# Transposes among the products, a later place for the softmax transposes, and a stage change that awaits no store

## What is computed

```python
x = L0_attn_x
xn = _layernorm(x, axis=-1)
s = _L0_attn_ref(xn, ...)          # four heads of 128 columns, concatenated, @ warboss_w + warboss_b
g = _silu(_L0_ffn_ref(xn, ...))    # relu(xn @ w1 + b1) @ w2 + b2, w1: 512x2048, w2: 2048x512
x = x + s * g

def _full_attention(x, qkv_w, scale):            # local head
    qkv = x @ qkv_w
    q, k, v = jnp.split(qkv, 3, axis=-1)
    scores = jnp.einsum('bsh,bth->bst', q, k) * scale
    probs = jax.nn.softmax(scores, axis=-1)
    return probs @ v
# sparse head: the same, but scores below the row's 102nd largest are masked before the softmax
# memory head: softmax(x_proj @ bank.T) over 64 entries, then [x_proj, retrieved] @ mem_out_w + b
# prediction head: two linear layers, exact gelu, one linear layer
```

## Time and profile before

| | us |
|---|---|
| median of 3 runs (2620.21 to 2622.47) | 2621.97 |
| the profiled execution | 2622.3 |
| its span in the profile | 2620.5 |
| TensorE busy | 2536.6 (97%) |
| VectorE busy | 2308.1 (88%) |
| ScalarE busy | 1367.2 (52%) |
| GpSimd busy | 1101.9 (42%) |

### The profile page before, as it was taken

How to read it: one execution, slowest core, us unless ns; L and a number is a source line. 1 busy time by engine, 2 the same in 40 slices (tenths; PEclk the granted TensorE clock), 3 DMA queues, 4 the chain that set the end, 5 groups by cost and what they waited for, 6 DMA issues and landing times.

```text
span 2620.5 us, 37059 instructions
## 1 busy us (share of the span) xinstructions
PE 2536.6 (97%) x12900; PEld 2145.1 (82%) x12900; DVE 2308.1 (88%) x5217; ACT 1367.2 (52%) x2311; POOL 1101.9 (42%) x863
## 2 busy tenths in 40 slices
PE   6999999969999999999999999999999999999998
PEld 5887888857888888888888888888888888888886
DVE  7555555569999999999999999999999999999996
ACT  5777777734444445444444444544455444445443
POOL 4444444423344444444444444444444444444444
PEclk9999999989999999999999999999999999999999
DMA  6777777794556455655664556456655655475554
GB/s 215 291 291 296 286 273 273 291 349 145 195 185 239 164 193 197 227 175 195 203 232 162 193 199 227 165 197 216 209 183 179 239 187 199 164 243 175 196 169 166
DMA packets 168554, 562.29 MB, mean 215 GB/s; under 512 B 18160, under 2 KB 31664, under 8 KB 159920
## 3 DMA queue, kind: packets, MB, share of 16 engines
q1 hardware_dynamic: 168368, 559.91, 61.1%
HBM read 425.63 MB, written 134.22 MB: 214 GB/s over the span
## 4 chain that ended last, share of the span: by engine, by line
PE 75%; DVE 2%; DMA 1%; POOL 0%; issue 0%; ACT 0%; SPq 0%; POOLq 0%
PE acc L58 9%; PE acc L59 9%; PE acc L60 9%; PE hid L60 9%; PE hid L58 9%; PE hid L59 9%; PE o L58 4%; PE o L60 4%; PE o L59 4%; PE scores L1250 4%; PE scores L60 2%; PE scores L58 2%; PE scores L59 2%; DVE larger L1166 1%; DVE top_l L1146 1%; DMA xnT<-xnT_scratch 0%
## 5 line engine op out<-in xcount | busy, mean ns | idle before, releaser
L1006 POOL TENSOR_TENSOR h_lo<-h,h_hi 128x512 fp32r<-128x512 f32 x256 | 332.5, 1299 | 876.0 <-ACT h_hi L904 874.9
L1146 DVE MAX8 top_l<-larger 128x8 f32<-128x512 f32 x832 | 573.9, 690 | 13.2
L1166 DVE MATCH_REPLACE8 larger<-top_l,larger 128x512 f32<-128x512 f32 x768 | 519.3, 676 | 0.0
L903 ACT ACTIVATE h<-hid,b 128x512 f32<-128x512 f32 x256 | 176.4, 689 | 484.5 <-PE hid L60 484.0
L58 PE MATMUL acc<-w2s,h_hi 128*128 128x512 f32 x1024 | 411.7, 402 | 0.0
L58 PE MATMUL hid<-xnT,w1s 128*128 128x512 f32 x1024 | 399.6, 390 | 4.9 <-DMA w1s<-ffn_scratch 2.0
L59 PE MATMUL acc<-w2s,h_hi 128*128 128x512 f32 x1024 | 400.3, 391 | 0.0
L60 PE MATMUL acc<-w2s,h_lo 128*128 128x512 f32 x1024 | 400.3, 391 | 0.0
L60 PE MATMUL hid<-xnT,w1s 128*128 128x512 f32 x1024 | 399.8, 390 | 0.0
L59 PE MATMUL hid<-xnT,w1s 128*128 128x512 f32 x1024 | 399.0, 390 | 0.0
L1006 POOL TENSOR_TENSOR pT_s<-pT,pT_s 128x512 fp32r<-128x512 f32 x256 | 326.3, 1296 | 50.9 <-ACT pT_s L916 50.9
(11 more groups left out here) (170 smaller groups left out, 5570.8 us busy)
## 6 DMA issues: line engine op xcount, KB each, us to landing
w2s<-ffn_scratch SPq DMA_DIRECT2D x259, 512.0 KB, 3.9
w1s<-ffn_scratch SPq DMA_DIRECT2D x258, 512.0 KB, 4.5
kv<-kv_scratch SPq DMA_DIRECT2D x34, 1024.0 KB, 6.6
xnT<-xnT_scratch SPq DMA_DIRECT2D x68, 512.0 KB, 7.6
tl<-tile_scratch SPq DMA_DIRECT2D x66, 512.0 KB, 3.9
xnT_scratch<-xnT SPq DMA_DIRECT2D x16, 2048.0 KB, 13.6
kv_scratch<-kv_out SPq DMA_DIRECT2D x32, 1024.0 KB, 5.6
tile_scratch<-tiles_out SPq DMA_DIRECT2D x16, 2048.0 KB, 7.7
```

The costliest lines, as they stand in the source:

```text
L903: nc.scalar.activation(h32[:, c % 2, :], hid[:, :], ACT.Relu, bias=bias)
L1006: return nc.gpsimd.tensor_tensor(out_, value, hi_.bitcast(F32), ALU.subtract).then_inc(ready, 1)
L1146: l_step = count(nc.vector.max(top_l[:, own], larger[:, :]))
L1166: l_step = count(nc.vector.match_replace(larger[:, :], top_l[:, own], larger[:, :], LOWEST))
```

## The change

**Stage 1.** `JOBS` has a new order: `tr0` stands behind `ql`, `tr1` behind `qs`, `tr2` behind `kl`, and `wt` behind `ks`. Each of these four jobs of transposes is woven into the last three matmuls of the job before it: one transpose before them, one in each of the two gaps, one behind. VectorE makes `gelu_lo` before it splits the result of `wt`. The last step drops the load and the layer norm of a half batch that nobody reads and the load of an `ffn` chunk; VectorE makes the last low part of `v23` in GpSimd's place.

**The change of stages.** `xnT`, and one buffer each for the first tile, the sparse head's keys and the first `w1` chunk, are now shared by both stages. Stage 2 finds its first `xnT` half there, and the three others are loaded in the last step of stage 1, before its last two stores. SyncE waits for the landing of the `xnT` stores only at the end of stage 1; for `tile_scratch` and `kv_scratch` it waits inside stage 2, in front of the loads that read them (`load_kv` of the local keys, `load_tl`) or later. Further loads of `xnT` are issued one slot later.

**Stage 2.** `f2` takes the transposes and puts one behind the first and one behind the second of the three matmuls of each product, eight in all. `tr_done` now counts halves, and ScalarE waits for each half. The last group of all stays as it was.

```diff
-JOBS = ["mp", "pi", "ql", "ms", "p1a", "p1b", "qs", "wt", "kl", "ks", "p2",
-        "tr0", "tr1", "tr2", "tr3", "mo", "v01", "v23"]
+JOBS = ["mp", "pi", "ql", "tr0", "ms", "p1a", "p1b", "qs", "tr1", "kl", "tr2", "ks", "wt", "p2", "tr3", "mo",
+        "v01", "v23"]
+WOVEN = {"ql": "tr0", "qs": "tr1", "kl": "tr2", "ks": "wt"}
...
+def woven(nc, out, w_hi, w_lo, x_hi, x_lo, first, last, between):
+
+    nc.tensor.matmul(out, w_hi, x_hi, start=first, stop=False)
+    next(between, None)
+    nc.tensor.matmul(out, w_hi, x_lo, start=False, stop=False)
+    next(between, None)
+    return nc.tensor.matmul(out, w_lo, x_hi, start=False, stop=last)
...
-    LO = ["xp", "pin", "wt", "gelu"]
+    LO = ["xp", "pin", "gelu", "wt"]
...
+                def load_first():
+
+                    sp.wait_ge(kv_st, 32 * LAST)
+                    sp.wait_ge(tiles_st, 16 * LAST)
+                    loads = ((shared.tl0[:, :, :, :].rearrange("p i s n -> p (i s n)"),
+                              tile_d[0, :, :, :, :].rearrange("p i s n -> p (i s n)")),
...
+                    for (to, of), ready in zip(loads, shared.first_in):
+                        sp.dma_start(to.bitcast(F32), of).then_inc(ready, 16)
...
+                        if n == LAST:
+                            load_first()
...
-                        load_ffn((n + 1) & (CH - 1))
-
-                        sp.wait_ge(kv_l, 4 * n + 4)
+                        if n < LAST:
+                            load_ffn(n + 1)
+                            sp.wait_ge(kv_l, 4 * n + 4)
+                        else:
+                            sp.wait_ge(kv_l, 4 * n + 3)
+                            sp.wait_ge(last_v_l, 1)
                         store_kv(2)
...
                 sp.wait_ge(xnT_st, 16 * 2 * B)
-                sp.wait_ge(kv_st, 16 * 4 * B)
-                sp.wait_ge(tiles_st, 16 * 2 * B)
-                sp.wait_ge(ffn_st, 16 * 2 * B)
-                sp.wait_ge(ffn_in, 32 * (2 * B + 1))
...
+                                if name in WOVEN:
+                                    between = one_by_one(n, WOVEN[name])
+                                    next(between)
+                                    last = woven(nc, dst, wp_hi[:, k, c], wp_lo[:, k, c], xnT[:, hh, k, HI, :],
+                                                 xnT[:, hh, k, LOW, :], False, True, between)
+                                    last.then_inc(job_done, 1)
+                                    next(between)
+                                    continue
...
-                load_tl(0, 0, 0)
-                load_kv(U_KS, 0)
-                load_w1(0, 0)
-                load_xn(0, 0, 0)
                 load_w1(1, 1)
+                sp.wait_ge(tiles_st, 16 * 2 * B)
+                load_w2(0, 0)
                 load_kv(U_KL, 0)
-                for c in range(W2_RING - 1):
-                    load_w2(c, c)
+                load_w2(1, 1)
                 load_tl(1, 1, 1)
+                sp.wait_ge(kv_st, 16 * 4 * B)
...
                     i = 2 * g + t
-                    act.wait_ge(tr_done, i + 1)
                     for j in range(2):
+                        act.wait_ge(tr_done, 2 * i + j + 1)
...
-                        last = product(nc, acc[:, t, :], h_hi[:, c % 2, t * P:(t + 1) * P],
-                                       h_lo[:, c % 2, t * P:(t + 1) * P], w2[:, r, HI, :], w2[:, r, LOW, :],
-                                       start, c % CH == CH - 1)
+                        last = woven(nc, acc[:, t, :], h_hi[:, c % 2, t * P:(t + 1) * P],
+                                     h_lo[:, c % 2, t * P:(t + 1) * P], w2[:, r, HI, :], w2[:, r, LOW, :],
+                                     start, c % CH == CH - 1, between)
```

More of the change, by code:

```diff
@@ L13 @@
 from contextlib import ExitStack
+from dataclasses import dataclass
 import concourse.bass as bass
@@ L554, in transposes, with one_by_one @@
                     return last
+                def one_by_one(n, name):
+                    bk = bank(n, name)
+                    free = bank_free(n, name)
+                    if free is not None:
+                        pe.wait_ge(bank_read, free)
+                    if name == "wt":
+                        pe.wait_ge(wn_ready, n + 1)
+                    elif name == "tr0":
+                        pe.wait_ge(xn_ready, n + 2)
+                    for t in range(HTILES):
+                        source = we[:, t, :, :] if name == "wt" else xn[:, t, int(name[2]) * P:(int(name[2]) + 1) * P]
+                        last = nc.tensor.transpose(ps[:, bk, t * P:(t + 1) * P], source, ident[:, :])
+                        if t == HTILES - 1:
+                            last.then_inc(job_done, 1)
+                        yield last
                 pe.wait_ge(consts, CONSTS)
@@ L648, in _, with stage2 @@
                     steps(b)
-def stage2(nc, x, xnT_d, kv_d, tile_d, ffn_d, ident, ww_hi, ww_lo, b2, half_bias, b1, out):
+def stage2(nc, x, xnT_d, kv_d, tile_d, ffn_d, shared, out):
+    ident, ww_hi, ww_lo = shared.ident, shared.ww_hi, shared.ww_lo
+    b2, half_bias, b1 = shared.b2, shared.half_bias, shared.small[:, 0:CH]
+    xnT = shared.xnT
     HC = CH // HTILES
@@ L668, in sem @@
             return ctx.enter_context(nc.semaphore(name))
-        xnT = sb("xnT", [P, 2, KT, 2, HALF], F32R)
-        kv = sb("kv", [P, 8, 2, HALF], F32R)
-        tl = sb("tl", [P, TL_RING, 2, 4, P], F32R)
-        w1 = sb("w1s", [P, W1_RING, 2, D], F32R)
+        values = sb("values", [P, 4, 2, HALF], F32R)
         w2 = sb("w2s", [P, W2_RING, 2, D], F32R)
+        kl = sb("kl", [P, 2, 2, HALF], F32R)
+        units = {U_KS: shared.ks, U_KL: kl, U_VL: values[:, 0:2, :, :], U_VS: values[:, 2:4, :, :]}
+        tl = [shared.tl0] + [sb(f"tl{j}", [P, 2, 4, P], F32R) for j in range(1, TL_RING)]
+        w1 = [shared.w10, sb("w1_1", [P, 2, D], F32R)]
         h32 = sb("h32", [P, 2, HALF], F32)
@@ L1347, in slots @@
                             pe.wait_ge(pl_ready, m + 1)
[L1348 to L1349 removed]
+                            f2(C + 1, c + 1, h, transposes(0))
                             f1(C + 3, c + 3, h)
```

185 lines of the change are left out of this document (110 added, 75 removed).

## The result

The changed kernel takes 2657.3 us (2656.4 to 2659.7), the kernel before on the same chip 2621.1 us: a ratio of 1.0141, 95% interval 1.0123 to 1.0158. It is slower by 36 us, outside the predicted range of 2594 to 2636; the forecast was 2621.2, no change. The profiled execution has a span of 2654.6 us, against 2620.5 before, so 34.1 us are to be found in the two traces.

A forecast was written before the change was run, and what follows sets the result against it. TensorE was taken as the bound, always busy in stage 2, with 22.0 us of stage-1 waits and 17.2 us between stages. 2622.3 + 8.2 - 14.4 + 5.1 = 2621.2 us, range 2594 to 2636.

The forecast's parts named there:

- Part 1: Stage 1: the wait for `we` goes, a 1.9 us wait at `mo` comes; +8.2 us, bounds 0 and +16.
- VectorE's 0.69: Stage 1: VectorE's subtraction on the `wt` result, ahead of `mo`, was taken to last 0.69 us.
- rival D: Stage 1: the wait in front of `mo` lets TensorE's clock fall, 16 x 1.6 = 26 us more, 2647; chance 0.09.
- Part 2: Change of stages: the gap shrinks until transfers become the limit; -14.4 us, bounds -10 and -17.2.
- E+20.6: Change of stages: summed transfers let the second-chunk `w1` product start 20.6 us after TensorE's stage-1 end, 14.3 us earlier.
- keep its length: Early stage 2: the chain through ScalarE's `prob` and TensorE's 4.24 us idle before the transposes stay as long, only moving earlier.
- first `kv` store of the sum: Change of stages: the transfer sum starts with this store, issued 7.3 us before TensorE's end of stage 1.
- Part 3: Stage 2: weaving transposes between products gains nothing, 0.04 us more for each of 127 groups; +5.1 us, bounds -4 and +13.
- The argument for the group: Stage 2: each transpose leaves one weight load bare, eight in a row or woven; group 3.68 us for 3.64.
- Rival B: Stage 2: weaving pays, a woven transpose costs only its columns; 50 us less, 2566; chance 0.09.
- Rival C: Stage 1: the new wait at `mo` does not come, so the 22.0 us are saved; 2592; chance 0.12.

The follow-up runs named there:

- the kernel with 1.69 us: Changed kernel with TensorE's wait at `mo` put behind the three products of `mo` that do not need its result: 2640.3 us.
- e3_old_jobs: Changed kernel with stage 1 in its old job order and nothing woven there; stage change and stage 2 kept: 2620.6 us, 0.9997 of before.
- e10_before_wt_behind_kl: Kernel before with `wt` one place later, behind `kl`, and `gelu_lo` ahead of it on VectorE: 2594.9 us, 0.9904 of before.

## Why the prediction was wrong

**Part 1, stage 1: the wait moved as forecast, and two terms of its price failed.** Stage 1 was to cost 8.2 us and cost 40.1. The two terms are VectorE's subtraction, put at 0.69 us, and the fall of the clock, put at nothing in the forecast. The forecast had the wait for `we` go and one at `mo` come. Its path holds nearly to the end. Counted from the step's start at 297.21, ScalarE begins `qs` at 16.29 (forecast 16.26), VectorE begins its subtraction at 320.69 - 297.21 = 23.48 (23.4), and TensorE reaches `mo` at 322.26 - 2.47 - 297.21 = 22.58 (22.4). The first term that failed is "VectorE's 0.69": it was 1.42, because the later `wt` meets GpSimd's `ks`. 0.73 more there make the result come at 25.05 instead of 24.27, the wait 2.47 instead of 1.9, and a step with full clock 32.42 instead of 31.64. Over 16 steps this is 12.5 us of the miss. The 0.69 was read from a row in which GpSimd was all but done. Its timeline there:

```profile
325.81 1.29 POOL L315 TENSOR_TENSOR tiles_out<-tiles_out 128x512 fp32r<-128x512 f32 x1 [6.13 <-ACT tiles_out L408]
```

It ends at 327.10, 0.11 us after VectorE's start. The trace of before had the warning in its groups by line and form (busy, mean ns of one). Two groups of subtractions of one shape cost 929 and 690 ns on the mean: half of the first meet a running operation of GpSimd and take up to 1.54 us, none of the second does:

```profile
L447 DVE TENSOR_TENSOR xnT<-xnT 128x512 fp32r<-128x512 f32 x56 | 49.9, 929 | 64.8 <-ACT xnT L433 64.8
...
L447 DVE TENSOR_TENSOR act_lo<-act,act_hi 128x512 fp32r<-128x512 f32 x30 | 20.7, 690 | 14.4 <-ACT act_hi L378 14.4
```

**The second term is the clock: rival D had the mechanism and was given 0.09.** It put 1.6 us on a fall; 1.5 was measured, 13 times instead of 16, some 19 us, and its sign, a granted clock under 1.00 in stage 1, is there (0.96). The step that failed was to set the point of decision between 1.4 and 4.24 us and then weigh it as if it lay near the upper end. Nothing between the two had been seen, so a wait of 1.9 was an open case, and the kernel with 1.69 us shows that the clock would have fallen about every second time. With a wait that long and a fall in half of the steps, the forecast of 2621 would have been some 12 us too low even without VectorE's 0.73.

**Part 2, the change of stages: nearly right.** Forecast -14.4, bounds -10 and -17.2. The timeline of TensorE in the changed kernel, which answers to the earlier trace rows:

```profile
569.95 0.56 PE L60 MATMUL scores<-ks,tl 128*128 128x512 f32 x1 [2.95 <-PEq L228]
...
580.01 0.47 PE L60 MATMUL hid<-xnT,w 128*128 128x512 f32 x1 [4.11 <-DMA w<-ffn_scratch]
...
587.84 0.50 PE L60 MATMUL hid<-xnT,w 128*128 128x512 f32 x1 [0.52 <-DMA w<-ffn_scratch]
...
623.25 0.79 PE L67 MATMUL acc<-w2s,h_hi 128*128 128x512 f32 x1 [5.59 <-ACT prob L1030]
```

TensorE ends stage 1 at 567.0, the forecast's E. The product that was summed up to E+20.6 stands at 587.84, E+20.8 (it opens the third chunk of the hidden layer and not the second, in both kernels). Behind it the wait for `prob` is 5.6 and not the 4.24 that was to "keep its length", and up to the fifth slot 13.3 us are won. In e3_old_jobs, whose stage 1 is that of before, it is only 9.6, just outside the bounds. There TensorE waits 5.1 us for `ks` and 4.0 for `w1`, and the former is shorter in the changed kernel (2.95). SyncE's timeline of the changed kernel has the reason, and it makes the hit at E+20.6 a lucky one:

```profile
557.31 0.36 SPq L305 DMA_DIRECT2D kv_scratch<-kv_out  x1
```

This is the first `kv` store of the sum, 9.7 us before E; the forecast said 7.3, and in e3_old_jobs it is 6.4. From it to the product at the end of the sum it is 30.5 us in both kernels, and 27.9 in the forecast. So the transfers took 2.6 us longer than they were summed to, and the stores had 2.4 more of a start, because E itself was put off by the late subtraction and the fall of the clock (0.8 and 1.5 us).

**Part 3, the weaving: right in sign and in the group, low in sum.** Forecast +5.1, upper bound +13; the 28 pairs show +8.3, the kernel without weaving 7 us less. The group of 8 and 12 was to take 3.68 and takes 3.68. What was left out lies behind it: in the 12 products of the next chunk the 11 distances add up to 0.038 us more, 2.531 for 2.493 on the mean of 87 groups from 1000 to 2400 us, and 4 groups per pair to 0.15 of the 0.30. The argument for the group, one bare load for each transpose wherever it stands, gives the right number and is not the whole mechanism, since pairs of transposes cost less. **Rival B** (2566) found no support: a woven transpose cost 0.12 us. The Trainium skill (TensorE: Matmul & The Clock Gate, Back-to-back issue gap) gives 81 ns for a sustained 128-column LDWEIGHTS and MATMUL. These traces do not agree: 0.115 us in a row and 0.12 woven. **Rival C** was out as soon as `mo` waited at all, and it was priced too low: with no wait in stage 1 the gain is 26 us (e10_before_wt_behind_kl), not 22.

**The sum by its terms**: stage 1 +8.2, measured +40.1; change of stages -14.4, measured -13.3; weaving +5.1, measured +8.3; -1.1 behind the last whole pair, which no term of the forecast has. The change of stages with a stage 1 that moves `wt` by one place, and no weaving, brings 33 us instead (2620.5 - 2587.7).

## What to carry to other kernels

A job that is moved later to spare one wait has to be followed to its reader, and the distance to that reader is worth more than the wait spared: `wt` one place later, behind `kl`, gained 26 us in the old order, and in the new order `wt` behind `ks` instead of inside `kl` lost 35 (2657.3 - 2622.3). Price an operation of VectorE on such a path by what GpSimd does at its new moment, not by its own best row; and price a new standstill of TensorE at its length from start to start plus one fall of the clock, unless the trace shows equal waits that cost none. Before a producer is moved on one engine, read the whole order of the queue that stores its result: a late operation ahead of a store delays every store behind it.

## What the runs showed of the hardware

- VectorE's subtraction of two SBUF operands (64x512) took 0.69 us with GpSimd idle, 1.42 and 2.14 when it began inside a GpSimd subtraction, and ended 0.54 to 0.56 us behind that one's end. With 0.11 us of GpSimd's operation left it still took 0.69.
- The same wait of TensorE can cost the clock or not: 1.69 us did so in 8 of 15 cases, nearly by turns, 2.44 us in 12 of 15, 1.45 us in none. Each fall was one stretch at 1.2 GHz that cost 1.5 to 1.6 us. What decides between equal waits is not shown here.
- Idle products in front of a wait were worth their time: nine of them, 2.0 us of work for nothing in each step, made the kernel 17 us faster, as the clock stayed at 2.4 GHz.
- A transpose of 128 columns between two products of 512 costs 0.12 us and in a row of eight 0.115; its cost shows on the instruction behind the next one.
